# One transformer layer on one core: the projections of q and k from whole float32 products to products of two float32r parts

## What is computed

```python
Xn = (X - mu) * rsqrt(var + EPS) * ln_g + ln_b
Q, K, V = (split_heads(Xn @ W + b) for W, b in ((Wq, bq), (Wk, bk), (Wv, bv)))
scores = where(causal, einsum('bhqd,bhkd->bhqk', Q, K) / sqrt(16), -inf)
x = layernorm(X + (softmax(scores) @ V) @ Wo + bo)
h = relu(x @ W1 + b1)
alpha = softmax(h @ W2 + b2)                      # 8 weights for each row
y = layernorm(x + sum_k alpha_k * U_k @ (V_k @ x))
```

## Time and profile before

| | |
|---|---|
| median of three runs | 436.98 us (436.42 to 437.85) |
| the profiled execution, time | 436.52 us |
| the profiled execution, span of its instructions | 434.8 us |
| busy: TensorE, VectorE, ScalarE, GpSimd | 407.4, 309.3, 241.3, 74.6 us |
| mean granted TensorE clock | 0.994 |

### The profile page before, as it was taken

How to read it: one execution, slowest core, us unless ns; L and a number is a source line. 1 busy time by engine, 2 the same in 40 slices (tenths; PEclk the granted TensorE clock), 3 DMA queues, 4 the chain that set the end, 5 groups by cost and what they waited for, 6 DMA issues and landing times.

```text
span 434.8 us, 7330 instructions
## 1 busy us (share of the span) xinstructions
PE 407.4 (94%) x2563; PEld 214.1 (49%) x2563; DVE 309.3 (71%) x805; ACT 241.3 (55%) x535; POOL 74.6 (17%) x111
## 2 busy tenths in 40 slices
PE   7997899999989999999999999999999998998994
PEld 3545444353324445467757844335433444447683
DVE  4638997798798756627478799789879864214665
ACT  5691554766766667542541265567666758552321
POOL 4331210233121010111331021113312011010000
PEclk9999999999998999999999999999999999999999
DMA  6066761450402000000775037145040000000011
GB/s 194 8 100 97 192 96 26 62 85 5 74 1 99 0 3 0 0 2 0 157 132 76 3 77 105 16 67 84 2 75 3 0 3 0 2 0 2 1 48 50
DMA packets 18452, 21.14 MB, mean 49 GB/s; under 512 B 4976, under 2 KB 11888, under 8 KB 18416
## 3 DMA queue, kind: packets, MB, share of 16 engines
q1 hardware_dynamic: 18365, 20.66, 25.5%
q10 hardware_dynamic: 51, 0.01, 0.0%
HBM read 5.79 MB, written 2.10 MB: 18 GB/s over the span
## 4 chain that ended last, share of the span: by engine, by line
PE 71%; DVE 17%; ACT 7%; issue 2%; POOL 1%; DMA 1%; POOLq 0%; DVEq 0%; ACTq 0%
PE ps L881 16%; PE ps L995 14%; PE ps L975 14%; PE ps L952 10%; DVE mx L771 9%; PE ps L889 7%; PE ps L897 2%; PE ps L872 2%; DVE ps L767 2%; ACT pr L641 2%; PE ps L956 2%; PE ps L1005 2%; PE ps L1046 1%; DVE st L704 1%; ACT stk L568 1%
## 5 line engine op out<-in xcount | busy, mean ns | idle before, releaser
L641 ACT ACTIVATE pr<-ps 128x512 f32<-128x512 f32 (+3 forms) x384 | 166.0, 495 | 96.9 <-PE ps L975 95.4
L771 DVE TENSOR_REDUCE mx<-ps 128x1 f32<-128x512 f32 (+3 forms) x240 | 145.7, 666 | 15.1 <-PE ps L952 7.8
L975 PE MATMUL ps<-stq,stk 99*128 99x512 bf16 (+3 forms) x384 | 116.6, 331 | 4.6 <-ACT pr L641 3.3
L952 PE MATMUL ps<-stk,stq 96*128 96x512 bf16 (+3 forms) x384 | 113.2, 328 | 2.1 <-DVE mx L771 0.9
L559 POOL TENSOR_SCALAR_AFFINE_SELECT pr<-pr 128x512 f32<-128x512 f32 x64 | 40.9, 639 | 255.4 <-ACT pr L641 255.4
L995 PE MATMUL ps<-pr,va 128*32 128x512 f32 (+3 forms) x768 | 82.4, 501 | 0.5 <-POOL pr L559 0.5
L975 PEld LDWEIGHTS ps<-stq,stk 99*128 99x128 bf16 x384 | 34.5, 98 | 91.0 <-ACT pr L641 51.8
L952 PEld LDWEIGHTS ps<-stk,stq 96*128 96x128 bf16 x384 | 37.7, 98 | 23.4 <-issue 7.4
L767 DVE CUSTOM_DVE_ANT_0 ps<-ps,causal 128x384 f32<-128x384 f32 (+1 forms) x64 | 38.6, 647 | 11.6 <-PE ps L952 11.6
L956 PE MATMUL ps<-mask,ident_b 128*128 128x128 bf16 x192 | 35.5, 220 | 0.0
L881 PE MATMUL ps<-u_t,avt 128*128 128x256 f32 x128 | 30.7, 382 | 0.2 <-ACT avt L663 0.2
(11 more groups left out here) (95 smaller groups left out, 385.6 us busy)
## 6 DMA issues: line engine op xcount, KB each, us to landing
stq<-qk_raw SPq DMA_DIRECT2D x32, 96.0 KB, 2.8
stk<-qk_raw SPq DMA_DIRECT2D x32, 96.0 KB, 2.8
x_in<-in_x SPq DMA_DIRECT2D x8, 256.0 KB, 3.9
stq<-qk_raw SPq DMA_DIRECT2D x32, 64.0 KB, 2.4
stk<-qk_raw SPq DMA_DIRECT2D x32, 64.0 KB, 2.4
out_y<-x SPq DMA_DIRECT2D x3, 512.0 KB, 3.0
stk<-qk_raw SPq DMA_DIRECT2D x32, 32.0 KB, 2.4
stq<-qk_raw SPq DMA_DIRECT2D x32, 32.0 KB, 2.2
```

The costliest lines, as they stand in the source:

```text
L641: nc.scalar.activation(probs(b, g, s)[:, j, q0 - c * CHUNK:], act_bank(ev)[:, q0 - c * CHUNK:], ACT.Exp, scale=DH ** -0.5).then_inc(s_act_ ...
L771: nc.vector.tensor_reduce(dst, src, AX.X, ALU.max).then_inc(s_dve_free, 1)
L952: last = nc.tensor.matmul(bank[:, i * w:(i + 1) * w], q[0:ROWS, t // TPC, j, tile(t % TPC)], k[0:ROWS, k0 // CHUNK, j, 0:w], start=True, s ...
L975: nc.tensor.matmul(bank[:, q0 - c * CHUNK:], stk[stack_of(b, g)][0:ROWS + PARTS, kt // TPC, j, tile(kt % TPC)], stq[stack_of(b, g)][0:ROWS ...
```

## The change

- The weights of q and k are loaded whole into the space of `o_t`, and at the head of the program ScalarE makes their near parts (`halve`) and GpSimd their far parts (`far`), each one instruction of 512 columns for a side.
- `xt` now has ScalarE write the near float32r part of both halves first, then the whole `xt` of both halves (four instructions for a chunk, not two); the bank is freed by the whole copy, which stays because v reads it. GpSimd then subtracts: one instruction for each half gives the far part.
- A `qk` product is six float32r matmuls (L889's helper) in place of two float32 ones. The first pair (b, c, m) = (0, 0, 0) issues the near products of q and k ahead of the wait for the far part of `xt`.
- The far parts of W1 and V go from VectorE to GpSimd, at the same places of the order.
- RES is 2, not 3.
- `constant_rows(1)` stands behind `constant_rows(0)`; `(2)` and `(3)` stand before the copies of v for tiles 4 and 6.
- VectorE's wait for the masks goes from the head to the first instruction that reads the mask.
- At the change of batches one map product `u` and the transposes `ot` of batch 0 come ahead of the first `qk` of batch 1.
- Some tiles are smaller or shared (`flat`, `va`, `alpha`), which makes room for the new ones.

```diff
-RES = 3
+RES = 2
...
-    order = ([("load", 0)] + [("ln1", 0, c * TPC, TPC) for c in range(C)] + begin(0, 0) + [("stack", 0, 1, 0)]
+    order = ([("load", 0), ("ln1", 0, 0, TPC)] + [(e, 0, w, None) for w in "qk" for e in ("halve", "far")]
+             + [("ln1", 0, c * TPC, TPC) for c in range(1, C)] + begin(0, 0) + [("stack", 0, 1, 0)]
...
-            order += qk[:1] + ot + m[0][8:10] + [r4, r6, n] + qk[1:2] + m[0][10:11] + qk[2:3] + [("load", nb)] + turned
+            order += m[0][8:9] + ot + qk[:1] + m[0][9:10] + [r4, r6, n] + qk[1:2] + m[0][10:11] + qk[2:3] + [("load", nb)] + turned
...
-        w_qk = sb("w_qk", [P, KC, 2, D])
+        w_qk = sb("w_qk", [P, 2, 2, KC, D], F32R)
...
-        flat = sb("flat", [P, 2 * D + E])
+        flat = sb("flat", [P, D + E])
...
-        va_rows = sb("va", [P, T, HEADS * (DH + 1) + VW])
+        va_rows = sb("va", [P, T, HEADS * (DH + 1) + VW - DH - 1])
...
-        alpha = sb("alpha", [P, C, TPC, E])
+        alpha = le
...
+        xt_parts = sb("xt_parts", [P, 2, KC, CHUNK], F32R)
...
+        whole_q, whole_k = (o_t[:, i, :].rearrange("p (k d) -> p k d", d=D) for i in range(2))
+        split_weights = {"1": (whole_1, w_1), "vt": (whole_vt, v_t), "q": (whole_q, w_qk[:, :, 0]), "k": (whole_k, w_qk[:, :, 1])}
...
+        def xt_part(b, c, i):
+            return (xt_parts if b or c == 0 else x1_t)[:, i]
...
     @block.sync
-                            weight(w_qk[:, :, 0, :], wq, "qk")
-                            weight(w_qk[:, :, 1, :], wk, "qk")
+                            weight(whole_q, wq, "q")
+                            weight(whole_k, wk, "k")
...
-                        sp.dma_start(flat[:], rows.partition_broadcast(P)).then_inc(s_flat, 16)
+                        sp.dma_start(flat[:], rows[D:].partition_broadcast(P)).then_inc(s_flat, 16)
...
     @block.gpsimd
+                if kind == "far":
+                    _, _, name, k = ev
+                    whole, split = split_weights[name]
+                    pool.wait_ge(s_weight_near, n_halve["halve", *ev[1:]])
+                    k = slice(None) if k is None else k
+                    pool.tensor_tensor(split[:, 1, k], whole[:, k], split[:, 0, k].bitcast(F32),
+                                       ALU.subtract).then_inc(s_weight_far, 1)
+                if kind == "xt":
+                    _, _, c, k = ev
+                    pool.wait_ge(s_act_free, n_act[ev])
+                    if b and c:
+                        pool.wait_ge(s_dve_full, n_dve["qk", b, KC - 1, 0, 1])
+                    pool.tensor_tensor(xt_part(b, c, 1)[:, k], xt[:, c, k, :], xt_part(b, c, 0)[:, k].bitcast(F32),
+                                       ALU.subtract).then_inc(s_xt_far, 1)
...
     @block.scalar
             constant_rows(0)
+            constant_rows(1)
...
                     if ev == quick[0]:
-                        constant_rows(1)
                         act.wait_ge(s_cols, 16)
-                if kind == "v" and b == 0 and ev[2] in (0, 2):
-                    constant_rows(2 + ev[2] // 2)
+                if kind == "v" and b == 0 and ev[2] >= TPC:
+                    constant_rows(ev[2] // 2)
                 if kind == "halve":
                     _, _, name, k = ev
                     whole, split = split_weights[name]
+                    k = slice(None) if k is None else k
                     act.wait_ge(s_w[name], 16)
...
-                if kind in ("xt", "ot", "h"):
+                if kind == "xt":
                     _, _, c, k = ev
                     act.wait_ge(s_act_full, n_act[ev])
-                    if kind == "xt":
-                        ins = nc.scalar.activation(xt[:, c, k, :], act_bank(ev), ACT.Identity,
-                                                   scale=cols[:, 0, k:k + 1], bias=cols[:, 1, k:k + 1])
...
+                    normed = {"scale": cols[:, 0, k:k + 1], "bias": cols[:, 1, k:k + 1]}
+                    nc.scalar.activation(xt_part(b, c, 0)[:, k], act_bank(ev), ACT.Identity, **normed).then_inc(s_xt_near, 1)
+                    if k == KC - 1:
+                        for i in range(KC):
+                            normed = {"scale": cols[:, 0, i:i + 1], "bias": cols[:, 1, i:i + 1]}
+                            nc.scalar.activation(xt[:, c, i, :], act_bank(("xt", b, c, i)), ACT.Identity, **normed).then_inc(s_act_free, 1)
...
     @block.vector
-            dve.wait_ge(s_mask, 6)
...
-                if kind == "far":
-                    _, _, name, k = ev
-                    whole, split = split_weights[name]
-                    dve.wait_ge(s_weight_near, n_halve["halve", *ev[1:]])
-                    nc.vector.tensor_tensor(split[:, 1, k], whole[:, k], split[:, 0, k].bitcast(F32),
-                                            ALU.subtract).then_inc(s_weight_far, 1)
...
                     if on_vector(g, units[u]):
+                        dve.wait_ge(s_mask, 6)
...
     @block.tensor
                 if kind == "qk":
                     _, _, m, c, w = ev
-                    bank = take_dve(ev)
-                    weights("qk", b, 32)
-                    product(bank, lambda k: w_qk[:, k, w, tile(m)], lambda k: xt[:, c, k, :], KC,
-                            lambda k: ("xt", b, c, k)).then_inc(s_dve_full, 1)
+                    def sides(ev):
+                        _, b, m, c, w = ev
+                        return lambda i, k: w_qk[:, i, w, k, tile(m)], lambda j, k: xt_part(b, c, j)[:, k]
+
+                    ahead = (b, c, m) == (0, 0, 0)
+                    for one in [ev, (*ev[:4], 1)] if ahead and w == 0 else [] if ahead else [ev]:
+                        pe.wait_ge(s_xt_near, n_xt["xt", b, c, KC - 1])
+                        if b == 0:
+                            pe.wait_ge(s_weight_far, n_far["far", 0, "qk"[one[4]], None])
+                        part_products(take_dve(one), *sides(one), ((0, 0), (1, 0)), KC, start=True)
+                    pe.wait_ge(s_xt_far, n_xt["xt", b, c, KC - 1])
+                    part_products(dve_bank(ev), *sides(ev), ((0, 1),), KC, stop=True).then_inc(s_dve_full, 1)
```

21 lines of the change are left out of this document (15 added, 6 removed).

## The result

The changed kernel is slower: 441.87 us in the median of 20 runs (438.85 to 444.60) against 437.87 us of the kernel before, measured beside it (20 runs, 434.72 to 441.26). The ratio is 1.0097, with a 95% interval of 1.0071 to 1.0123. Every ratio in this document leaves out runs more than 1.5% above the fastest of the same kernel. The prediction said 435.5 us, 432.8 to 438.7, and is wrong.

A forecast was written before the change was run, and what follows sets the result against it. TensorE was taken as the usual bound, 71% of the chain. Middle -3.3, start -0.35 and change of batches +1.0 gave -2.65 us; one clock fall of 1.2 made it -1.45, so 435.5 us median, range 432.8 to 438.7.

The forecast's parts named there:

- Part 1: Projections on TensorE: six float32r matmuls take 1.48 us against 1.72, 0.24 for each of 16 products, 3.9 us in all.
- Part 2: Batch 0's attention: W1 and V far parts leave VectorE, the split's wait shortens and the clock holds; -3.3 us.
- Part 3: Start, up to the last residue: new order walked with row durations, last residue 31.05 instead of 31.39; -0.35 us.
- The ring and the bank: Start: residues wait for the low part two before, 1.16 us of GpSimd; the first bank is free 1.32 later.
- the 0.49 us split: VectorE's `L787` beside a GpSimd cut took 0.49 us, mean 0.195, ending about when the cut ended.
- Part 4: Change of batches: later bank and ring of two outweigh faster products; +1.0 us, bounds -1.9 and +2.0.
- The bank wait: Change of batches: TensorE waits 2.4 us instead of 0.63 before `h`, for a bank ScalarE's copies hold.
- Part 5: Clock: one of the two new TensorE waits, 2.2 and 2.4 us, lowers the clock; +1.2 us.
- The slower case: Change of batches: the whole copies' bank makes TensorE wait, two clock falls add 3.4 us; 438.9 us, chance 0.13.
- GpSimd holding VectorE: Middle: a far part meeting the split costs up to 1.0 us, bringing part 2 to -1.2; no chance of its own.
- another case: Both-fall rival: the clock falls behind both new waits, at the start and the change of batches; 436.7 us, chance 0.15.
- two signs of being wrong: Prediction wrong if batch 0's stretch keeps a late split, or if TensorE's waits of 2.2 and 2.4 us are absent.

The follow-up runs named there:

- a1: Kernel before with only the far parts of W1 and V moved from VectorE to GpSimd; ratio 0.9962 to the kernel before.
- d1: Changed kernel with ScalarE's middle part of batch 1's first product moved ahead of the two root instructions; ratio 1.0116 to the kernel before.
- c2: Changed kernel with q/k far weights on VectorE, three residue buffers, twelve filling matmuls, alternating near/whole copies, middle part ahead of roots; ratio 0.9909 to the kernel before.
- c4: Kernel before with two added GpSimd memsets of 128x1024 float32 that nothing reads, begun at the first root; run once for its trace, last residue at 32.12 us.
- a4: Changed kernel with twelve useless matmuls ahead of the third v tile, to fill TensorE's wait; ratio 1.0089 to the kernel before.
- b1: Changed kernel with q/k weights' far parts on VectorE and twelve filling matmuls at the start; ratio 1.0010 to the kernel before.
- b2: Changed kernel with q/k weights' far parts on VectorE, twelve filling matmuls at the start and three residue buffers; ratio 0.9963 to the kernel before.
- a2: Changed kernel with the far parts of q's and k's weights made on VectorE, not GpSimd; ratio 1.0108 to the kernel before.
- a3: Changed kernel with three buffers of residues instead of two; ratio 1.0015 to the kernel before.
- b3: Changed kernel with the order at the change of batches as it was before; ratio 1.0121 to the kernel before.
- b4: Changed kernel with ScalarE's copies of xt in the order near, whole, near, whole; ratio 0.9997 to the kernel before.
- d2: Changed kernel with q/k far weights on VectorE, filling matmuls, alternating copies and middle part ahead of roots, but two residue buffers; ratio 0.9981 to the kernel before.
- c3: Kernel before with two added GpSimd subtractions of 128x512 float32 that nothing uses, begun at the first root; run once for its trace, last residue at 34.74 us.

## Why the prediction was wrong

**Part 1 was right in size** (0.25 us a product) and **Part 2 was right in its stretch**: -3.3 forecast, -3.27 measured, with the split's wait and the clock as said. Attention of batch 0 as a whole gave 2.90. As a term of the whole time it was too large: it counted 1.7 us of clock as gained for good, and in a1 a fall elsewhere took them back.

**Part 3 failed.** It walked the last residue to 31.05; it came at 35.70. The walk took every instruction of VectorE at its duration from before, and placed GpSimd's new far parts beside them as if the two engines were apart. Two held stretches were missing: the norm of chunk 0, 3.42 for 1.38 us, and the small chain of chunk 1, 1.16 + 1.18 for 0.32, together 4.1 us. The first has its test in d1: with 1.09 us less of it, the first residue and the v product came 1.09 earlier. The second stands in every repaired kernel too (0.50 and 1.14 us in c2), so no run took it away; its price rests on the trace, and on c4, where a longer norm reached the last residue in full. Without both the first residue, at 17.95, would have waited only for its product, at 14.3 in the walk. ScalarE came to the copies of chunk 1 at 23.14 instead of 20.2, and TensorE waited 3.02 us instead of 2.2. Of the 4.65 us, about 3.0 are this delay and 1.65 the low clock, which the prediction priced apart. The ring and the bank were in the walk already. The text had the right row for it, the 0.49 us split, and named the lock, but looked for a meeting only at the split in the middle. The trace of the kernel before even has it in a chain of four-column instructions, in its timelines of GpSimd and VectorE, 0.48 us where the others take 0.16:

```profile
178.02 0.65 POOL L559 TENSOR_SCALAR_AFFINE_SELECT pr<-pr 128x512 f32<-128x512 f32 x1 [17.94 <-ACT pr L641]
...
178.20 0.48 DVE L696 SCALAR_TENSOR_TENSOR nv<-nv 128x4 f32<-128x4 f32 x1
```

One bound of this part was also added up wrong: 3.8 less 2.6 is 1.2, not 1.5; nothing in the outcome hangs on it.

**Part 4 was undersized**, +1.0 against +2.19 (just past the bound of 2.0). The `h` product was walked to 212.6, which is 213.3 here, as this execution came to the end of batch 0's attention 0.7 us later; it came at 214.20, and 0.77 of the 0.9 is the held norm. The order edit had been followed on TensorE and VectorE, but not on ScalarE, where it let the roots pass the middle part. The prediction also used the low part's old start, 223.28, though it had itself made the chain 0.75 late: the third residue was walked to 224.4 and came at 227.03. The bank wait was right in place and a little high in size (2.4 against 1.99).

**Part 5 was right in kind and low in price.** One of the two waits lowered the clock in the profiled execution, as forecast, at 1.65 us instead of 1.2. Which wait it follows the prediction could not say. In the eight profiled executions with a wait of about 2.0 us before `h`, the clock fell there in four (a4, b1, b2, d1), all of which had kept 1.00 at the start, and held there in the four in which it had fallen at the start (changed, a2, a3, b3). That is a pattern of eight executions, and its cause was not tried. Some of the 20 runs seem to have more falls: the mean granted clock is 0.994 or 0.995 in seven of the 20, with spans of 436.6 to 437.8, and 0.984 in four, with 441.2 to 442.2. The median lies 1.8 us above the profiled execution, where 0.46 was added.

By the sum: -1.45 forecast, +2.90 measured in span, a miss of 4.35. The start makes 2.7 of it (+3.59 against -0.35 and the fall's 1.2), the change 1.2, the middle 0.4. Another 0.7 lies outside the span, 440.10 - 437.7 = 2.4 us where it was 1.7; it is 2.2 to 2.4 in all 20 runs, and no run here explains it.

**The rivals.** The slower case had its time from the whole copies' bank at the change and two falls of the clock. The bank wait is there, and copies in turn take back 1.24 us (b4), but it was neither the largest part nor did it decide: the step from batch 0's last score (187.49 us before, 188.17 after) to batch 1's first grew from 63.1 to 65.3 us, not by 5. The rival that was true, GpSimd holding VectorE, stood inside another case at no chance of its own. The prediction's two signs of being wrong, a late split and missing waits, did not appear either: they tested what it had walked, not VectorE at the start, which it had taken as given.

**What cost how much**, by the repairs: at the start the clock 1.1 to 1.65, the ring 1.1 to 1.3 and the weights' far parts 0.7; the copies in turn brought the last residue 0.5 (b4 against a4) to 1.4 us (c2 against b2) forward. At the change the copies' order 1.24, the ring 0.7 to 1.05 (a3, d2, b2 against b1), the held norm 0.74. All together take the start from 47.19 to 42.85 and the change from 66.85 to 64.27 (c2).

## What to carry to other kernels

When work goes to GpSimd, list what VectorE does in the same microseconds, down to its smallest instructions. Here the norms, the small chains and the split, whose tensors all lie in SBUF, were held by a GpSimd instruction that reads SBUF until its end; row maxima and residues, which read PSUM, and the batch statistics were not. So add what is left of GpSimd's instruction for each meeting of the first kind, and move the work, if you can, beside the second. In a chain of small dependent instructions every meeting counts in full. When an order is moved, follow it on every engine, for a part that merely changed sides with a tiny instruction can land beside the wrong neighbour. And a faster engine that has to wait for its old neighbour may lose more in its clock than it gained: fill the wait or shorten the hold of what it waits for, before making it faster.

## What the runs showed of the hardware

- A GpSimd subtraction of 128x512 float32 held a four-column VectorE instruction from 0.16 to 1.04 us (c3), and also ones with a single tensor input (1.09 and 1.18 us in a2). A GpSimd memset let four-column instructions with two tensor inputs pass at 0.16, but held a 128x256 instruction with one from 0.40 to 1.11 us (c4). Residues, at 0.75 us, and batch statistics, four in 1.39, were not held by subtractions (changed kernel, d1). The SBUF — State Buffer page of the Trainium skill (two separate sides) describes a pair of ports that the two engines share as an exclusive lock, held for the whole instruction, and lets a VectorE instruction with two SBUF inputs meet it only against a GpSimd one that reads SBUF. By that rule, c3's rows agree, and so do the four-column ones of c4.
- The clock is not settled by the length of a wait alone: behind 3.02 and 3.03 us of idle TensorE in the same place it fell in one execution and not in the other, and behind 1.98 to 2.00 us at the change it held in the changed kernel, a2, a3 and b3 and fell in a4, b1, b2 and d1. With the wait at the start filled, a4, b1 and b2 had their fall at the next long one; c2, where that one was 1.32 us, had none there.
- One fall cost 1.65 us of the chain where TensorE was the bound (changed kernel against d1, from 23 to 36 us).
